# Cross-attention with a quantised feed-forward layer: three engines' attention loops written out, and each head's key loads cut in halves

## The chip, the cores and the metric

The kernel runs on one core of one Trainium2 chip. The core has five engines that work side by side, each with an instruction queue of its own: TensorE (PE in the profile) for matrix products, VectorE (DVE), ScalarE (ACT), GpSimd (POOL) and SyncE (SP), which here only issues DMAs. The engines wait for each other through semaphores. Sixteen DMA engines move data between DRAM and the on-chip memory, and they also do transposes on the way. The metric is the device time of one execution in microseconds (us). Less is better.

## The reference

With layer-normalised input x (4 x 512 tokens, 512 channels) and a context of 4 x 1601 = 6404 rows:

```python
q = (x @ Wq + bq).reshape(1, B * N, H, hd)            # 2048 queries, 16 heads of 32
kv = (cond @ Wkv + bkv).reshape(1, -1, 2, H, hd)      # 6404 keys and values
q = _fq_sym(q * scale, axis=-1)                       # to 8 bits and back, per query
k = _fq_sym(k, axis=-1)                               # per key
v = _fq_sym(v, axis=2)                                # per channel over all keys
attn = softmax(einsum('bhqd,bhkd->bhqk', q, k))
attn = _fq_unsigned(attn, axis=-1)                    # to 0..255 by the row's maximum, and back
out = einsum('bhqk,bhkd->bhqd', attn, v) @ Wp + bp
x = x + out
x = x + ffn(layernorm(x))                             # block-quantised, 512 -> 2048 -> 512
```

Every query attends to all 6404 keys.

## The kernel before

It has three stages: weights, queries, keys and values are made and written to DRAM; then `attention`; then `finish`, which is the output projection and the feed-forward layer. Only `attention` is changed.

**The unit of work** is a row: one head and one tile of 128 queries, against all 6404 keys. There are 16 heads (`H`) of 16 rows (`QT`), so 256 rows, and head h works on rows 16h to 16h + 15. Below, "row 5 of a head" counts from 0. What happens to a row:

1. TensorE makes the scores (L732), in five chunks (`NCH`) of 1280 or 1281 keys. The keys are held in three bf16 parts stacked to 96 partitions (`k_parts`, two slots: one for the head at work, one for the next), the queries likewise (`q_rep`).
2. VectorE copies each chunk out of the two PSUM buffers to `s_row` and takes its maximum in the same pass (L784). There are two `s_row` buffers, so row r + 2 waits until the exponents of row r are done.
3. GpSimd combines the five maxima and makes the bias of the exponent (L884 to L901).
4. ScalarE takes the exponent in two halves (L836): 3328 keys as bytes, 3076 as 16-bit integers.
5. SyncE issues two DMA transposes (`turn`): L711 for the byte half, L717 for the other.
6. GpSimd unpacks the transposed bytes in two casts (L909, L910), after it has done the maxima of the following row.
7. TensorE multiplies by the values (L745). This is put between the score chunks of the row three later (`LAG` = 3), in program order. ScalarE copies the result out (L842).

**Loads for the next head** are all issued by ScalarE, in `next_head`, between the exponents of its rows. `load` (L807 to L811) brings one of three key parts, all 6404 keys of 32 channels, and the queries for the same partitions; `load_values` brings the values in three pieces. Steps 0 to 2 (`load`) come in rows 2 to 4, steps 3 to 5 (`load_values`) in rows 5 to 7. Heads 1 to 14 do this for heads 2 to 15; heads 0 and 1 are loaded at the start, the values of head 1 in row 5 of head 0. TensorE's first row of a head waits for `head_loaded`, which counts 16 for each of six DMAs (L760). GpSimd scales and rounds the new values (`scale_values`, `round_values`) in three parts in its rows 8 to 13; TensorE waits for them in row 3 of their head (L765).

**Loops.** VectorE's part is written out in full. TensorE has one loop inside each head (L767), and that stays. ScalarE writes out heads 0, 1, 14 and 15 and loops over pairs of heads between (L871). GpSimd writes out head 0 and loops over pairs of heads, from an odd one on (L969), with a loop over the first eight rows inside (L939). SyncE loops over pairs of rows (L721). `settle` only increments a semaphore that nobody waits for.

Of the kernel before, what the change touches and what calls it, by code (L numbers as in the profile page):

```python
# [17 lines left out]
ds = bass.ds  # L18
# [601 lines left out]
def attention(nc, A, arena, q_dram, k_dram, v_dram, scales, v_scale, attn, zinv, wp, vectors, wp_loaded):  # L620
# [40 lines left out]
    VP = 3  # L661
# [3 lines left out]
    with Phase(nc, "a") as ph:  # L665
# [38 lines left out]
        def _(sp):  # L704
            def turn(pair, u):
                row = pair * 2 + u
                after_first(sp, unpacked, row - 1)
                settle(sp, sp_passed)
                sp.wait_ge(exp_done[0], row + 1)
                settle(sp, sp_passed)  # L710
# [3 lines left out]
                settle(sp, sp_passed)  # L714
                sp.wait_ge(exp_done[1], row + 1)
                settle(sp, sp_passed)
                sp.dma_start_transpose(nT[:, u, HALF_TILES:KT], n16[:, u, :].bitcast(FP16)).then_inc(turned[u][1], 16)  # L717

            turn(0, 0)
            turn(0, 1)  # L720
            with sp.Fori(1, PAIRS) as pair:  # L721
                for u in range(2):
                    turn(pair, u)

        @block.tensor
        def _(pe):
# [32 lines left out]
            def rows_of_head(h, slot, loaded):  # L759
                pe.wait_ge(head_loaded[slot], loaded * 96)  # L760
# [42 lines left out]
        def _(act):  # L803
# [18 lines left out]
            def next_head(h, slot, step):  # L822
# [22 lines left out]
            def rows_of_head(h, slot, last=False):  # L845
                for t in range(QT):
# [4 lines left out]
                    if not last and 2 <= t < 8 and not (isinstance(h, int) and h == 0):  # L851
                        next_head(h + 1, 1 - slot, t - 2)
# [5 lines left out]
            for s in range(3):  # L858
                load(0, 0, s)
# [3 lines left out]
            for s in range(3):  # L863
                load(1, 1, s)
# [15 lines left out]
        def _(pool):  # L880
            def take_scales(row, u):
                after_first(pool, exp_done[1], row - 1)
                settle(pool, pool_passed)
                nc.gpsimd.tensor_copy(row_scale[:, u, :], scales[:, row % QT, row // QT, :]).then_inc(scale_ready, 1)  # L884

            def maximum(row, u):
# [3 lines left out]
                settle(pool, pool_passed)  # L890
# [4 lines left out]
                settle(pool, pool_passed)  # L895
# [4 lines left out]
                settle(pool, pool_passed)  # L900
# [3 lines left out]
            def unpack(row, u):  # L904
# [3 lines left out]
                settle(pool, pool_passed)  # L908
# [8 lines left out]
            def scale_values(h, part):  # L917
                if part == 0:
                    pool.wait_ge(raw_loaded, h * 64 + 64)
                    settle(pool, pool_passed)  # L920
# [4 lines left out]
            def round_values(h, v_slot, part):  # L925
# [3 lines left out]
                settle(pool, pool_passed)  # L929
# [4 lines left out]
            PP = QT // 2  # L934
            BEFORE = 4

            def rows_of_head(h, slot):

                with pool.Fori(0, BEFORE) as i:  # L939
                    for u in range(2):  # L940
                        maximum_and_unpack(h * QT + (2 * i + u), u)
                for part in range(VP):
                    maximum_and_unpack(h * QT + 2 * (BEFORE + part), 0)
                    scale_values(h + 1, part)
                    maximum_and_unpack(h * QT + 2 * (BEFORE + part) + 1, 1)
                    round_values(h + 1, 1 - slot, part)
                for i in range(BEFORE + VP, PP):
                    for u in range(2):
                        maximum_and_unpack(h * QT + (2 * i + u), u)

            def first_rows():
                for row in range(2 * BEFORE):
                    maximum_and_unpack(row, row % 2)
                for part in range(VP):
                    maximum_and_unpack(2 * (BEFORE + part), 0)
                    scale_values(1, part)
                    maximum_and_unpack(2 * (BEFORE + part) + 1, 1)
                    round_values(1, 1, part)
# [514 lines left out]
```

## Time and profile before

| | |
|---|---|
| median of 3 runs | 2925.6 us |
| lowest, highest | 2914.03, 2931.51 us |
| the profiled execution | 2919.24 us |
| its span, first to last instruction | 2917.4 us |
| busy: VectorE, TensorE, ScalarE, GpSimd | 2513.0, 2268.8, 1993.3, 1400.3 us |
| DMA packets | 1420697, of them 1377512 under 512 B |

The profile comes from one execution. The span is cut into stretches or groups of instructions, and for each the busy time of an engine is given, and, in front of an instruction, how long its engine stood idle and what ended that. "Issue" means that it waited for nothing that the profile shows. The clock is the share of TensorE's full clock that was granted.

### The profile page before, as it was taken

The page shows a single profiled execution, that of the slowest core. Times are in us where ns is not written, and L with a number is a line of the kernel's source. Part 1 is how long each engine was busy: PE and PEld are TensorE (multiplying, and loading weights), DVE is VectorE, ACT ScalarE, POOL GpSimd, SP SyncE. Part 2 cuts the span into 40 slices and gives each one's busy share as a digit, 9 for nine tenths or more (in the row PEclk, how much of TensorE's full clock was granted, in tenths as well). Part 3 has the DMA queues.
Part 4 walks back from the last instruction along what each step waited for, and adds up shares of the span by engine and source line. Part 5 has one row for each costly group of instructions (what it writes and reads, how often), then busy time and mean ns, then how long its engine had stood idle before and what let it go on. Part 6 is the DMA issues. An engine that isn't in the chain of part 4 may idle for free. (4 is left out here: it accounts for less than half of the span.)

```text
span 2917.4 us, 58686 instructions
## 1 busy us (share of the span) xinstructions
PE 2268.8 (78%) x20020; PEld 1192.2 (41%) x20020; DVE 2513.0 (86%) x3665; ACT 1993.3 (68%) x1859; POOL 1400.3 (48%) x1772
## 2 busy tenths in 40 slices
PE   0379999976778788888778777878877888767876
PEld 0234555532444444444344444444434444433333
DVE  8665666657999999999899999999989999957887
ACT  1113444435888888888788888888878788855554
POOL 0001111114666657667576575765756667653331
PEclk9699999985887777777776678777778677888989
DMA  6112323338999999999999999999999999980000
GB/s 239 67 27 99 110 97 126 108 106 159 168 212 177 194 197 176 204 188 189 188 174 194 166 197 200 176 202 190 181 187 173 192 197 182 180 219 4 15 15 26
DMA packets 1420697, 444.96 MB, mean 153 GB/s; under 512 B 1377512, under 2 KB 1392872, under 8 KB 1417872
## 3 DMA queue, kind: packets, MB, share of 16 engines
q1 hardware_dynamic: 1311664, 402.10, 68.0%
q10 hardware_dynamic: 108864, 40.92, 7.6%
q8 instruction: 67, 1.10, 0.2%
q14 instruction: 102, 0.84, 0.1%
HBM read 80.41 MB, written 43.77 MB: 43 GB/s over the span
## 5 line engine op out<-in xcount | busy, mean ns | idle before, releaser
L784 DVE TENSOR_SCALAR_CACHE_REDUCE arena<-a_ps_s 128x1281 f32<-128x1281 f32 (+1 forms) x1280 | 1828.6, 1489 | 87.3 <-PE a_ps_s L732 53.5
L836 ACT ACTIVATE arena<-arena,a_bias,a_row_scale 128x3328 uint8<-128x3328 f32 (+1 forms) x512 | 1560.0, 3048 | 301.3 <-POOL a_bias L901 264.2
L732 PE MATMUL a_ps_s<-arena,a_q_rep 96*128 96x512 bf16 (+2 forms) x3840 | 1239.4, 445 | 345.3 <-DVE arena L784 316.8
L745 PEld LDWEIGHTS a_ps_o<-a_v_head,a_nT 128*128 128x128 f16 x13056 | 526.7, 103 | 340.8 <-issue 184.3
L909 POOL CAST a_nT<-arena 128x1664 int16<-128x1664 uint8 x256 | 401.8, 1569 | 521.4 <-DMA arena<-arena 501.0
L732 PEld LDWEIGHTS a_ps_s<-arena,a_q_rep 96*128 (+1 forms) x3840 | 316.2, 110 | 788.4 <-DVE arena L784 433.2
L745 PE MATMUL a_ps_o<-a_v_head,a_nT 128*128 128x32 f16 x13056 | 519.6, 184 | 77.0 <-POOL a_nT L910 59.7
L910 POOL CAST a_nT<-arena 128x1664 int16<-128x1664 uint8 x256 | 402.8, 1573 | 0.0
L471 POOL TENSOR_TENSOR kv_parts<-kv_rest,kv_parts 128x512 bf16<-128x512 f32 (+1 forms) x51 | 59.0, 1156 | 578.9 <-ACT kv_parts L586 578.9
L591 ACT ACTIVATE kv_stage<-kv_ps_t 128x1024 bf16<-128x1024 bf16 (+1 forms) x51 | 51.4, 1007 | 204.8 <-PE kv_ps_t L508 204.8
L499 PE MATMUL kv_ps_k<-wkv,kv_ctxT 128*128 128x512 f32 (+1 forms) x408 | 185.3, 597 | 0.0
L499 PE MATMUL kv_ps_v<-wkv,kv_ctxT 128*128 128x512 f32 (+1 forms) x408 | 183.4, 592 | 0.0
L896 POOL TENSOR_SCALAR a_row_max<-a_row_max,a_part_max 128x1 f32<-128x1 f32 x256 | 92.1, 360 | 85.8 <-POOL a_row_max L891 42.4
L499 PEld LDWEIGHTS kv_ps_v<-wkv,kv_ctxT 128*128 128x128 f32 (+1 forms) x408 | 76.7, 188 | 98.4 <-issue 98.4
L559 DVE TENSOR_TENSOR kv_rest<-kv_kq,kv_parts 128x512 f32<-128x512 f32 (+1 forms) x51 | 35.3, 692 | 81.9 <-issue 81.9
L784 DVE DVE_READ_ACCUMULATOR arena<-a_ps_s 128x1 f32 x1280 | 105.6, 83 | 0.0
L499 PEld LDWEIGHTS kv_ps_k<-wkv,kv_ctxT 128*128 128x128 f32 (+1 forms) x408 | 73.4, 190 | 75.0 <-issue 74.9
L930 POOL TENSOR_SCALAR a_v_head<-a_v_raw 128x544 f16<-128x544 f32 x48 | 98.6, 2055 | 0.0
L836 ACT ACTIVATION_READ_ACCUMULATOR arena<-arena,a_bias,a_row_scale (+1 forms) x512 | 95.9, 187 | 0.0
L901 POOL TENSOR_SCALAR a_bias<-a_row_max,a_row_scale 128x1 f32<-128x1 f32 x256 | 66.6, 260 | 59.3 <-POOL a_row_max L896 58.6
L891 POOL TENSOR_SCALAR a_row_max<-a_part_max 128x1 f32<-128x1 f32 x256 | 93.2, 364 | 0.5
L369 PE MATMUL w_ps_t<-ident,arena 128*128 128x128 bf16 x128 | 12.3, 289 | 86.3 <-DVE arena L293 86.3
(157 smaller groups left out, 1946.5 us busy)
## 6 DMA issues: line engine op xcount, KB each, us to landing
arena<-k_parts_transposed ACTq DMA_DIRECT2D x48, 400.2 KB, 4.9
k_parts_transposed<-kv_stage SPq DMA_DIRECT2D x10, 1920.0 KB, 7.9
kv_ctx<-in_ctx_dram SPq DMA_DIRECT2D x10, 1280.0 KB
v<-arena SPq DMA_DIRECT2D x10, 1280.0 KB
arena<-in_L_ffn_W_dram SPq DMA_DIRECT2D x2, 4096.0 KB, 20.8
a_v_raw<-v ACTq DMA_DIRECT2D x32, 208.0 KB
a_q_rep<-q_transposed ACTq DMA_DIRECT2D x48, 128.0 KB, 5.8
a_v_raw<-v ACTq DMA_DIRECT2D x16, 384.0 KB
```

Of the source, the lines that this page charges most:

```text
L471: nc.gpsimd.tensor_tensor(parts[0:r, 2, :], rest1[0:r, :], parts[0:r, 1, :], ALU.subtract).then_inc(lo_ready, 1)
L499: last = nc.tensor.matmul(ps[0:r, u, :], ctxT[:, u, j, 0:r], wkv[:, j, col:col + C], start=(j == 0), stop=(j == CC - 1))
L732: last = nc.tensor.matmul(ps_s[:, b, n0:n0 + w], q, k_parts[0:3 * HD, slot, start[c] + n0:start[c] + n0 + w], start=True, stop=True)
L745: last = nc.tensor.matmul(ps_o[:, u, 0:HD], nT[:, u, j, :], v_head[:, v_slot, j, :], start=(j == 0), stop=(j == KT - 1))
L784: nc.vector.tensor_scalar(s_row[:, u, start[c]:start[c] + size[c]], ps_s[:, (u + c) % 2, 0:size[c]], 1.0, None, ALU.mult, ALU.max, accum_o ...
L836: nc.scalar.activation(out, s_row[:, u, keys_of_half[half]], ACT.Exp, scale=row_scale[:, u, 0:1], bias=bias[:, u:u + 1], accum_out=zsum[:, ...
L891: nc.gpsimd.tensor_scalar(m, part_max[:, u, 0:1], part_max[:, u, 1:2], part_max[:, u, 2:3], ALU.max, ALU.max).then_inc(three_done, 1)
L896: nc.gpsimd.tensor_scalar(m, m, part_max[:, u, 3:4], part_max[:, u, 4:5], ALU.max, ALU.max).then_inc(row_max_ready, 1)
L901: nc.gpsimd.tensor_scalar(bias[:, u:u + 1], row_max[:, u:u + 1], row_scale[:, u, 1:2], LN255, ALU.mult, ALU.add).then_inc(bias_ready, 1)
L909: nc.gpsimd.tensor_copy(low_T[u], bytes_T[:, u, :, 0])
L910: nc.gpsimd.tensor_copy(high_T[u], bytes_T[:, u, :, 1]).then_inc(unpacked, 1)
L930: nc.gpsimd.tensor_scalar(v_head[:, v_slot, part * VT:(part + 1) * VT, :], v_raw[:, part * VT:(part + 1) * VT, :], ROUND, ROUND, ALU.add, ...
```

## The change

The loops of ScalarE, GpSimd and SyncE in `attention` are replaced by plain Python loops, so that every row's instructions are written out, and the `settle` calls there go. `load` now moves one key part in two DMAs, keys 0 to 2561 (`MIDDLE` = `start[2]` = 2562) and keys 2562 to 6403; the queries go with the second. The six halves are issued in rows 0 to 5 of a head, one a row, and the three value loads in rows 6 to 8. `head_loaded` therefore counts nine DMAs (144). GpSimd's work on the values goes from rows 8 to 13 to rows 10 to 15 (`BEFORE` = 10).

```diff
             def turn(pair, u):
                 row = pair * 2 + u
                 after_first(sp, unpacked, row - 1)
-                settle(sp, sp_passed)
                 sp.wait_ge(exp_done[0], row + 1)
-                settle(sp, sp_passed)
...
-            turn(0, 0)
-            turn(0, 1)
-            with sp.Fori(1, PAIRS) as pair:
+            for pair in range(PAIRS):
                 for u in range(2):
                     turn(pair, u)
...
-                pe.wait_ge(head_loaded[slot], loaded * 96)
+                pe.wait_ge(head_loaded[slot], loaded * 144)
...
-            def load(h, slot, s):
-                act.dma_start(k_parts[s * HD:(s + 1) * HD, slot, :],
-                             k_dram[s, ds(h * HD, HD), :]).then_inc(head_loaded[slot], 16)
+            MIDDLE = start[2]
+
+            def load(h, slot, s, half):
+                keys = slice(0, MIDDLE) if half == 0 else slice(MIDDLE, K)
+                act.dma_start(k_parts[s * HD:(s + 1) * HD, slot, keys],
+                             k_dram[s, ds(h * HD, HD), keys]).then_inc(head_loaded[slot], 16)
+                if half == 0:
+                    return
                 act.dma_start(q_rep[s * HD:(s + 1) * HD, slot, :],
                              q_dram[ds(h * HD, HD), :]).then_inc(head_loaded[slot], 16)
...
                 if step == 0:
                     act.wait_ge(scores_ready, (h - 1) * (QT * NCH))
-                if step < 3:
-                    load(h, slot, step)
-                if step >= 3:
+                if step < 6:
+                    load(h, slot, step // 2, step % 2)
+                if step >= 6:
                     act.wait_ge(v_rounded, h * VP)
-                    load_values(h, step - 3)
+                    load_values(h, step - 6)
...
-                    if not last and 2 <= t < 8 and not (isinstance(h, int) and h == 0):
-                        next_head(h + 1, 1 - slot, t - 2)
+                    if not last and t < 9 and not (isinstance(h, int) and h == 0):
+                        next_head(h + 1, 1 - slot, t)
...
             for s in range(3):
-                load(0, 0, s)
+                for half in range(2):
+                    load(0, 0, s, half)
...
-            rows_of_head(0, 0)
-            rows_of_head(1, 1)
-            with act.Fori(1, H // 2 - 1) as hh:
-                for slot in range(2):
-                    rows_of_head(2 * hh + slot, slot)
-            rows_of_head(H - 2, 0)
-            rows_of_head(H - 1, 1, last=True)
+            for h in range(H):
+                rows_of_head(h, h % 2, last=(h == H - 1))
...
-            BEFORE = 4
-
-            def rows_of_head(h, slot):
-
-                with pool.Fori(0, BEFORE) as i:
...
+            BEFORE = 10
+
+            def rows_of_head(h):
+
+                for t in range(QT):
+                    maximum_and_unpack(h * QT + t, t % 2)
+                    part = (t - BEFORE) // 2
+                    if h + 1 < H and 0 <= part < VP:
+                        if t % 2 == 0:
+                            scale_values(h + 1, part)
+                        else:
+                            round_values(h + 1, (h + 1) % 2, part)
...
-            with pool.Fori(0, H // 2 - 1) as hh:
-                rows_of_head(2 * hh + 1, 1)
-                rows_of_head(2 * hh + 2, 0)
-            with pool.Fori((H - 1) * PP, H * PP) as pair:
-                for u in range(2):
-                    maximum_and_unpack(2 * pair + u, u)
+            for h in range(H):
+                rows_of_head(h)
             unpack(ROWS - 1, 1)
```

## Rows read from the trace of the kernel before

"..." marks rows left out. A timeline row is: start, duration (us), engine, line, operation, output <- input, count, and in brackets the idle time before it and what ended it. In rows of L784 alone the columns are: stretch, its length, VectorE's busy time, clock, DMA share, GB/s; the sum adds the stretches' lengths.

**Rows 1.** head of the page: span, and busy time of each engine

```profile
span 2917.4 us, 58686 instructions
PE 2268.8 (78%) x20020; PEld 1192.2 (41%) x20020; DVE 2513.0 (86%) x3665; ACT 1993.3 (68%) x1859; POOL 1400.3 (48%) x1772
```

**Rows 2.** stretches: us, busy us by engine, TensorE clock, DMA share, GB/s

```profile
...
662.90:2580.50 1917.60, 1526.34 (x16788) 821.33 (x16788) 1830.27 (x2561) 1592.71 (x1272) 1224.14 (x1626) 0.75 1.02 186
...
```

**Rows 3.** costliest groups by line

```profile
L784 DVE TENSOR_SCALAR_CACHE_REDUCE arena<-a_ps_s 128x1281 f32<-128x1281 f32 (+1 forms) x1280 | 1828.6, 1489 | 87.3 <-PE a_ps_s L732 53.5
L836 ACT ACTIVATE arena<-arena,a_bias,a_row_scale 128x3328 uint8<-128x3328 f32 (+1 forms) x512 | 1560.0, 3048 | 301.3 <-POOL a_bias L901 264.2
...
```

**Rows 4.** L784 alone, one stretch per head (head 15, and the sum of sixteen)

```profile
...
2466.47:2580.44 113.97, 113.71 (x162) 0.85 0.96 177
sum 1917.54, DVE 1830.21; mean DVE 114.39
```

**Rows 5.** L784 alone, rows 5 to 7 of heads 1 to 14

```profile
...
2139.96:2170.84 30.88, 21.62 (x31) 0.61 1.12 185
...
sum 355.45, DVE 302.47; mean DVE 21.61
```

**Rows 6.** L784 alone, rows 8 to 15 of heads 1 to 14

```profile
...
sum 804.61, DVE 799.98; mean DVE 57.14
```

**Rows 7.** L784 alone, row 1 of heads 3, 5, 7, 9, 11, 13

```profile
...
sum 50.34, DVE 43.05; mean DVE 7.18
```

**Rows 8.** timeline of head 12, row 2, and of VectorE three rows later

```profile
2131.94 1.60 SPq L711 DMA_TRANSPOSE arena<-arena  x1
2132.18 0.38 ACTq L808 DMA_DIRECT2D arena<-k_parts_transposed  x1
2134.87 6.54 SPq L717 DMA_TRANSPOSE a_nT<-arena  x1
2141.14 1.57 POOL L909 CAST a_nT<-arena 128x1664 int16<-128x1664 uint8 x1 [7.02 <-DMA arena<-arena]
...
2146.09 1.49 DVE L784 TENSOR_SCALAR_CACHE_REDUCE arena<-a_ps_s 128x1281 f32<-128x1281 f32 x1 [3.22 <-PE a_ps_s L732]
```

**Rows 9.** timeline: a row without loads, then one with value loads

```profile
1490.77 1.47 SPq L711 DMA_TRANSPOSE arena<-arena  x1
...
1494.78 1.57 POOL L909 CAST a_nT<-arena 128x1664 int16<-128x1664 uint8 x1 [1.25 <-DMA arena<-arena]
...
2414.61 0.37 ACTq L818 DMA_DIRECT2D a_v_raw<-v  x1
2414.92 1.98 SPq L711 DMA_TRANSPOSE arena<-arena  x1
...
2420.65 1.57 POOL L909 CAST a_nT<-arena 128x1664 int16<-128x1664 uint8 x1 [2.70 <-DMA arena<-arena]
```

**Rows 10.** DMA issues: count, KB each, us from issue to landing

```profile
arena<-k_parts_transposed ACTq DMA_DIRECT2D x48, 400.2 KB, 4.9
a_q_rep<-q_transposed ACTq DMA_DIRECT2D x48, 128.0 KB, 5.8
a_v_raw<-v ACTq DMA_DIRECT2D x16, 384.0 KB
```

**Rows 11.** timeline of head 5: GpSimd in its row 0, VectorE in row 2

```profile
1275.06 0.18 POOL L884 COPY a_row_scale<-scales 128x2 f32 x1 [3.38 <-issue]
...
1280.21 1.49 DVE L784 TENSOR_SCALAR_CACHE_REDUCE arena<-a_ps_s 128x1281 f32<-128x1281 f32 x1 [0.57 <-ACT arena L836]
```

**Rows 12.** timeline: first loads, first scores, VectorE's first stall

```profile
650.39 0.41 ACTq L808 DMA_DIRECT2D arena<-k_parts_transposed  x1
...
652.75 0.44 ACTq L810 DMA_DIRECT2D a_q_rep<-q_transposed  x1
...
660.23 1.04 PE L732 MATMUL a_ps_s<-arena,a_q_rep 96*128 96x512 bf16 x2 [19.70 <-DMA a_q_rep<-q_transposed]
...
691.89 1.49 DVE L784 TENSOR_SCALAR_CACHE_REDUCE arena<-a_ps_s 128x1281 f32<-128x1281 f32 x1 [14.76 <-ACT arena L836]
```

More of the change, by code:

```diff
@@ L863, in _ @@
             for s in range(3):
-                load(1, 1, s)
+                for half in range(2):
+                    load(1, 1, s, half)
             act.dma_start(wp[:], A.wp.rearrange("(j p) n -> p j n", p=P)).then_inc(wp_loaded, 16)
@@ L882, in take_scales @@
                 after_first(pool, exp_done[1], row - 1)
-                settle(pool, pool_passed)
                 nc.gpsimd.tensor_copy(row_scale[:, u, :], scales[:, row % QT, row // QT, :]).then_inc(scale_ready, 1)
@@ L889, in maximum @@
                 pool.wait_ge(scores_taken, row * NCH + 3)
-                settle(pool, pool_passed)
                 nc.gpsimd.tensor_scalar(m, part_max[:, u, 0:1], part_max[:, u, 1:2], part_max[:, u, 2:3],
@@ L894, in maximum @@
                 pool.wait_ge(three_done, row + 1)
-                settle(pool, pool_passed)
                 nc.gpsimd.tensor_scalar(m, m, part_max[:, u, 3:4], part_max[:, u, 4:5],
@@ L899, in maximum @@
                 pool.wait_ge(scale_ready, row + 1)
-                settle(pool, pool_passed)
                 nc.gpsimd.tensor_scalar(bias[:, u:u + 1], row_max[:, u:u + 1], row_scale[:, u, 1:2], LN255,
@@ L907, in unpack @@
                 after_first(pool, values_done, row - 1)
-                settle(pool, pool_passed)
                 nc.gpsimd.tensor_copy(low_T[u], bytes_T[:, u, :, 0])
@@ L919, in scale_values @@
                     pool.wait_ge(raw_loaded, h * 64 + 64)
-                    settle(pool, pool_passed)
                 tiles_of = v_raw[:, part * VT:(part + 1) * VT, :]
@@ L928, in round_values @@
                     pool.wait_ge(values_done, (h - 1) * QT)
-                settle(pool, pool_passed)
                 nc.gpsimd.tensor_scalar(v_head[:, v_slot, part * VT:(part + 1) * VT, :],
@@ L932, in round_values @@
                                         ALU.add, ALU.subtract).then_inc(v_rounded, 1)
-            PP = QT // 2
-            BEFORE = 4
-            def rows_of_head(h, slot):
-                with pool.Fori(0, BEFORE) as i:
-                    for u in range(2):
[L941 to L958, printed above, removed]
-                for row in range(2 * (BEFORE + VP), QT):
-                    maximum_and_unpack(row, row % 2)
+            BEFORE = 10
[8 more added lines that the diff above has]
+                            round_values(h + 1, (h + 1) % 2, part)
             nc.gpsimd.partition_all_reduce(v_scale[:], v_scale[:], P, bass.bass_isa.ReduceOp.max).then_inc(reduced, 1)
@@ L967, in _ @@
                 round_values(0, 0, part)
-            first_rows()
-            with pool.Fori(0, H // 2 - 1) as hh:
-                rows_of_head(2 * hh + 1, 1)
-                rows_of_head(2 * hh + 2, 0)
-            with pool.Fori((H - 1) * PP, H * PP) as pair:
-                for u in range(2):
-                    maximum_and_unpack(2 * pair + u, u)
+            for h in range(H):
+                rows_of_head(h)
             unpack(ROWS - 1, 1)
```

2 lines of the change are left out of this document (removed).

## Prediction

> **What bounds the kernel now.** I read the head of the page first [rows 1], then cut the execution into stretches. The attention stage, from VectorE's first to its last L784, holds 1917.60 of 2917.4 us, and VectorE is busy in it for 1830.27 [rows 2]. Only this stage is changed. Its work is 1280 passes of L784, five for each of 256 rows, and all the idle time in front of them is 87.3 us [rows 3]. ScalarE is next, with 3.05 us for each of two exponents a row. So the change can win back what VectorE idles, and no more, and the question is where those 87 us lie.
>
> For that I cut the stage by rows. Rows 8 to 15 of heads 1 to 14, 112 rows, take 804.61 us, 7.184 each [rows 6]. Head 15, during which nothing is loaded for a next head, takes 113.97, or 7.12 a row [rows 4]. That is the pace without trouble. Three places are off it:
>
> - Rows 5 to 7 of heads 1 to 14: 42 rows in 355.45 us. At 7.184 they would take 301.7, so 53.7 us are lost, 1.28 a row. In head 12 alone the three rows take 30.88 [rows 5].
> - Row 1 of the six odd heads from 3 to 13: 50.34 us for 43.1, so 7.2 lost [rows 7].
> - The start, once: VectorE waits 14.76 us for the first exponent [rows 12].
>
> **Why rows 5 to 7 are late.** ScalarE issues the three key loads in its rows 2, 3 and 4. The timeline of head 12 shows what one does. The byte transpose (L711) starts at 2131.94, the key load (L808) 0.24 us later, and GpSimd's unpack (L909), which waits for that transpose, starts at 2141.14: 9.20 us instead of the 4.01 of a row without loads [rows 8, 9]. The second transpose's issue is held for 6.54 us too. TensorE does this row's values between the scores three rows later (LAG = 3), in order, so the scores are late and VectorE waits 3.22 us [rows 8]. The DMA share of the stage is 1.02 [rows 2]: there is hardly a gap in which a load could hide. From that pair of numbers the transposes may be late by 9.20 - 3.22 - 4.01 = 1.97 us before VectorE feels it. The lost 1.28 us a row then mean a mean lateness of about 3.25 us in a key-load row.
>
> Value loads are issued in rows 5 to 7, and would hurt in rows 8 to 10, where nothing is lost [rows 6]. The largest, 384 KB [rows 10], gives 2420.65 - 2414.92 = 5.73 us from transpose to unpack [rows 9], 1.72 over the quiet row and inside the allowance.
>
> **Part 1, key loads in halves.** Before, each of three rows carries 400.2 + 128.0 = 528 KB of keys and queries [rows 10]. MIDDLE is 2562 of 6404 keys. Now rows 0, 2, 4 carry 160 KB and rows 1, 3, 5 carry 240 + 128 = 368 KB. I take lateness as proportional to bytes. Light rows: 0.30 x 3.25 = 1.0 us, inside the allowance, cost nothing. Heavy rows: 0.70 x 3.25 = 2.3 us, 0.3 over. The lateness varies, though. The worst first load, in head 12, has 9.20 - 4.01 = 5.19 us [rows 8, 9], which becomes 3.6 and loses 1.7, while mild ones lose nothing. I take 0.45 us for each of 42 heavy rows: 19 us left of 53.7, a gain of 35. The bounds: the value load of 384 KB lost nothing, so 368 KB may lose nothing either, a gain of 53.7; or the same bytes lose the same time wherever they lie, a gain of 0.
>
> A rule of the Trainium skill speaks against the halves: "DMA: Bandwidth & Descriptors", section "Bandwidth", says to batch DMAs and that small ones are inefficient, and its section on the anatomy of one DMA gives a fixed part of about 2.0 us each (for those issued by GpSimd). Estimated from that page, 42 more DMAs are 84 us of transfer time, and were all of it on the path, the sum would end near 2962 and not near 2880. The rows show a whole 400 KB load landing in 4.9 us [rows 10], with VectorE at work meanwhile.
>
> **Part 2, no loops on GpSimd, ScalarE and SyncE.** In row 0 of head 5 GpSimd stands 3.38 us before L884 for no reason but issue, exactly where the loop over pairs of heads (L969) goes round; the exponents are late behind it, and VectorE waits 0.57 [rows 11]. Six heads show this, for 7.2 us together [rows 7]. Straight code has no such turn: -7.2. Its upper bound is that, its lower bound 0 if the pause comes again as a fetch of straight code. Against a pause in straight code: VectorE runs all its 1280 passes so, and of its 87.3 us of idle time [rows 3] the three places above explain 53.7 + 7.2 + 14.8, leaving 12 for 1280 passes. The removed settles (a semaphore increment each) stand on engines that wait for VectorE or the DMA anyway, GpSimd being busy 1224 of 1917.6 us [rows 2]: 0, covered by VectorE's passes; without that cover leaving them out could only gain. SyncE has run no long straight code here, so its term is bounded by 0 and by GpSimd's 3.38 us per pause, of which the allowance of 1.97 hides most; I take 0.
>
> **Part 3, values two rows later.** The three value loads go from ScalarE's rows 5 to 7 to 6 to 8, the scaling and rounding on GpSimd from rows 8 to 13 to rows 10 to 15. The rounded values are needed at row 3 of the next head (L765), more than two rows (14 us) after the last of them. Of the same work in the same kind of rows nothing is lost now [rows 6]: 0. ScalarE issues DMAs in nine rows a head and not in six, in light rows only one; its share of busy time, 1592.71 of 1917.6 us [rows 2], leaves 1.27 us a row, and the two issues of a heavy row take 0.38 + 0.44 [rows 8, 12].
>
> **Part 4, the start.** Head 0 now issues nine DMAs before the value loads. Six take 652.75 - 650.39 + 0.44 = 2.8 us, 0.47 each [rows 12]. Scores wait for the last query load, and the first exponent for the value loads behind it, so three more cost 1.4 us: +1.4. Between 0 and 2.8 if the issue of head 1's loads counts as well.
>
> **Sum.** -35 - 7.2 + 1.4 = -40.8 us against the profiled execution, 2919.24 us, of which 2917.4 are the span. That gives 2878. The median of the three runs is 2925.6, 6.4 above; I can't tell why, and if it is by more late transposes, the change takes those too; from there the sum gives 2885. I say 2880.
>
> **The rivals.** (a) All late rows vanish (0.20): 368 KB behaves as 384 KB of values do. Then -53.7 - 7.2 + 1.4 = -59.5, 2860 to 2866. Against it: by the code a value load moves pieces of 128 B and a key load pieces of 5 to 8 KB, and long pieces may hold up a transpose more than short ones. (b) Lateness follows the bytes however they are cut (0.16): the queue is full, so six rows lose what three lost. Then -5.8: 2913 to 2920. For it speaks the DMA share of 1.02; against it the value loads: 6404 x 32 x 4 bytes, 820 KB in three rows, follow the keys at once and lose nothing [rows 6]. (c) Slower (0.09): a key-load row loses 1.28 us whatever its size, because 32 key rows must pass between the transposes in each. Then 84 rows lose 107.4 us, +53.7 - 7.2 + 1.4 = +47.9: 2967 to 2974. It decides from 0.71 us per load row on ((53.7 + 5.8) / 84). The trace has key loads of one size only, so nothing there excludes it; the value loads, which also come in pieces over all engines, lose nothing, and speak against a price that any load pays. The forecast itself has 0.55, its own range 2868 to 2896.
>
> The range for eight in ten reaches from (a) to (b), 2858 to 2920; only (c) is outside. Half a per cent, 15 us, is about what measurement can tell from no change. Faster by more: the forecast, (a), and a small part of (b), 0.77; within: 0.14; slower: 0.09.
>
> **What would show it.** In the profile after: rows 3 to 8 of heads 1 to 14 lose about 19 us together, in rows 4, 6 and 8 (three after the heavy loads) and not 3, 5, 7; from byte transpose to unpack about 6.3 us in heavy rows, 5 in light ones; row 1 of odd heads at 7.1 to 7.2; the stage near 1877 us; rows 10 to 15 at 7.18. Wrong would be: pauses for issue on SyncE, GpSimd or ScalarE in front of L711, L884 or L836 in many rows; TensorE waiting at L765; or light rows as late as heavy ones.

## The result and the profile after

The changed kernel takes 2849.61 us (median of 4 runs, 2847.96 to 2854.95), the kernel before in the same comparison 2927.15 (4 runs, 2914.03 to 2931.51). The ratio is 0.9746, with a 95% interval of 0.9711 to 0.9780: faster, by 77.5 us. The forecast was 2880 with a range of 2858 to 2920. The direction was right, the size was not: the time lies 8 us below the low end of the range, and below what the most hopeful rival gave.

The page of the changed kernel, head, costliest groups and DMA issues:

```profile
span 2846.7 us, 54272 instructions
...
PE 2213.0 (78%) x20003; PEld 1185.6 (42%) x20020; DVE 2507.0 (88%) x3665; ACT 1993.3 (70%) x1859; POOL 1403.7 (49%) x1772
...
L778 DVE TENSOR_SCALAR_CACHE_REDUCE arena<-a_ps_s 128x1281 f32<-128x1281 f32 (+1 forms) x1280 | 1822.9, 1489 | 26.0 <-PE a_ps_s L726 10.6
L835 ACT ACTIVATE arena<-arena,a_bias,a_row_scale 128x3328 uint8<-128x3328 f32 (+1 forms) x512 | 1559.8, 3047 | 242.9 <-POOL a_bias L893 201.9
...
arena<-k_parts_transposed ACTq DMA_DIRECT2D x48, 240.1 KB, 3.8
...
arena<-k_parts_transposed ACTq DMA_DIRECT2D x48, 160.1 KB, 3.8
...
a_q_rep<-q_transposed ACTq DMA_DIRECT2D x48, 128.0 KB, 5.3
```

VectorE's 1280 passes are L778 now and not L784. They take 1822.9 us, 5.7 less than before, and the idle time in front of them is 26.0 us where it was 87.3 [rows 3]. So nearly all is in what VectorE waited for. The stage as one stretch:

```profile
660.10:2510.10 1850.00, 1475.38 (x16790) 814.73 (x16788) 1824.01 (x2561) 1592.73 (x1274) 1227.40 (x1626) 0.80 1.05 193
```

It is 1850.0 us long, 67.6 less than before [rows 2]. And cut by rows, L778 alone: first rows 5 to 7 of heads 1 to 14, second rows 3 to 8 of these heads (the rows that stand three behind a key load now), third their rows 9 to 15, fourth row 1 of the odd heads from 3 to 13. In each answer the sum stands last:

```profile
sum 306.73, DVE 299.29; mean DVE 21.38
...
sum 612.56, DVE 599.19; mean DVE 42.80
...
sum 699.95, DVE 697.86; mean DVE 49.85
...
sum 42.50, DVE 42.49; mean DVE 7.08
```

The same three stretches of the kernel before, where they were not shown yet (rows 3 to 8, rows 9 to 15):

```profile
sum 656.80, DVE 601.73; mean DVE 42.98
...
sum 704.18, DVE 700.21; mean DVE 50.02
```

From two such sums comes the measure that I use from here on. **Lost** is what the 84 rows 3 to 8 of heads 1 to 14 take above the pace of the 98 rows 9 to 15, in which nothing is late. Before: 656.80 - 84 x 704.18 / 98 = 53.2 us. After: 612.56 - 84 x 699.95 / 98 = 12.6. The 77.5 us are made up as follows, from the two profiled executions:

| where | before | after | difference |
|---|---|---|---|
| late rows ("lost") | 53.2 | 12.6 | -40.6 |
| row 1 of six odd heads | 50.34 | 42.50 | -7.8 |
| VectorE's first stall | 14.76 | 5.55 | -9.2 |
| rest of the stage (the pace falls from 7.186 to 7.142 us a row: 256 x 0.044 = 11) | | | -10.0 |
| ahead of the stage and behind it | 999.8 | 996.7 | -3.1 |
| span | 2917.4 | 2846.7 | -70.7 |

The remaining 7 us are that the profiled execution of before was 8 us faster than the median of its runs, and that of after 1 us faster. The first row is what I had forecast for part 1, within 6 us. The third had a term of the wrong sign, +1.4 (part 4), and the last two, 13 us, had none. Of these 13 us the experiments explain nothing: in a second profile of the changed kernel (g3 below) the pace is 7.163 us a row and not 7.142. It will turn out that the first row isn't what it seems either.

### The profile page after: what moved, and what is told of

It is laid out like the page before. It is cut to its first block and busy times, and to the rows that moved or that the text cites. A ratio compares the mean times of both kernels' runs of the same rounds, so it can differ in the third digit from the quotient of the medians.

```text
span 2846.7 us, 54272 instructions
## 1 busy us (share of the span) xinstructions
PE 2213.0 (78%) x20003; PEld 1185.6 (42%) x20020; DVE 2507.0 (88%) x3665; ACT 1993.3 (70%) x1859; POOL 1403.7 (49%) x1772
## 5 line engine op out<-in xcount | busy, mean ns | idle before, releaser
L778 DVE TENSOR_SCALAR_CACHE_REDUCE arena<-a_ps_s 128x1281 f32<-128x1281 f32 (+1 forms) x1280 | 1822.9, 1489 | 26.0 <-PE a_ps_s L726 10.6
L726 PE MATMUL a_ps_s<-arena,a_q_rep 96*128 96x512 bf16 (+2 forms) x3840 | 1186.6, 429 | 378.5 <-DVE arena L778 345.9
L726 PEld LDWEIGHTS a_ps_s<-arena,a_q_rep 96*128 (+1 forms) x3840 | 309.0, 108 | 809.5 <-DVE arena L778 460.5
L739 PE MATMUL a_ps_o<-a_v_head,a_nT 128*128 128x32 f16 x13056 | 512.6, 182 | 26.2 <-POOL a_nT L901 23.6
L559 DVE TENSOR_TENSOR kv_rest<-kv_kq,kv_parts 128x512 f32<-128x512 f32 (+1 forms) x51 | 35.3, 692 | 81.9 <-issue 81.9
L778 DVE DVE_READ_ACCUMULATOR arena<-a_ps_s 128x1 f32 x1280 | 106.3, 83 | 0.0
L835 ACT ACTIVATION_READ_ACCUMULATOR arena<-arena,a_bias,a_row_scale 128x1 f32 x512 | 95.8, 187 | 0.0
```

The lines of the kernel that those rows point to most:

```text
L726: last = nc.tensor.matmul(ps_s[:, b, n0:n0 + w], q, k_parts[0:3 * HD, slot, start[c] + n0:start[c] + n0 + w], start=True, stop=True)
L739: last = nc.tensor.matmul(ps_o[:, u, 0:HD], nT[:, u, j, :], v_head[:, v_slot, j, :], start=(j == 0), stop=(j == KT - 1))
L778: nc.vector.tensor_scalar(s_row[:, u, start[c]:start[c] + size[c]], ps_s[:, (u + c) % 2, 0:size[c]], 1.0, None, ALU.mult, ALU.max, accum_o ...
L835: nc.scalar.activation(out, s_row[:, u, keys_of_half[half]], ACT.Exp, scale=row_scale[:, u, 0:1], bias=bias[:, u:u + 1], accum_out=zsum[:, ...
```

## The experiments

Unless something else is said, a kernel is the changed one with the edit shown. "Before" is always the kernel before, run in the same comparison on the same chip. The last column is the mean time from the end of a row's last score pass on VectorE to the issue of its byte transpose, over rows 0 to 5 of heads 1 to 14.

| kernel | median us | before | ratio (95%) | first stall | lost | scores' end to transpose |
|---|---|---|---|---|---|---|
| before | 2927.15 | | | 14.76 | 53.2 | 7.61 |
| after | 2849.61 | 2927.15 | 0.9746 (0.9711 to 0.9780) | 5.55 | 12.6 | 5.59 |
| e1_loops_only | 2880.36 | 2918.17 | 0.9863 (0.9817 to 0.9910) | 5.37 | 35.3 | 5.71 |
| e2_loads_only | 2887.37 | 2918.17 | 0.9870 (0.9827 to 0.9912) | 12.9 | 30.8 | 7.25 |
| e3_whole_spaced | 2891.49 | 2918.17 | 0.9890 (0.9850 to 0.9929) | 5.58 | 47.7 | 6.56 |
| e4_queries_first | 2845.58 | 2918.17 | 0.9738 (0.9700 to 0.9775) | 5.02 | 2.0 | 5.24 |
| f5_settles_kept | 2871.51 | 2924.02 | 0.9830 (0.9789 to 0.9871) | 12.54 | 17.7 | 5.96 |
| f6_pool_loops | 2870.14 | 2924.02 | 0.9824 (0.9784 to 0.9864) | 13.63 | 14.2 | 5.77 |
| f7_act_loop | 2859.26 | 2924.02 | 0.9788 (0.9748 to 0.9827) | 5.07 | 20.0 | 6.20 |
| f8_sync_loop | 2857.73 | 2924.02 | 0.9775 (0.9735 to 0.9816) | 5.84 | 22.1 | 5.94 |
| g1_one_settle | 2860.24 | 2922.12 | 0.9797 (0.9754 to 0.9839) | 12.38 | 15.2 | 5.64 |
| g2_row_settles_twice | 2871.08 | 2922.12 | 0.9840 (0.9796 to 0.9885) | 6.04 | 25.8 | 6.39 |
| g3_after_again | 2852.59 | 2922.12 | 0.9770 (0.9737 to 0.9802) | 5.38 | 8.8 | 5.48 |
| g4_queries_first_again | 2844.48 | 2922.12 | 0.9746 (0.9713 to 0.9779) | 5.19 | 10.6 | 5.40 |
| h3_quiet_start | 2854.26 | 2929.16 | 0.9742 (0.9706 to 0.9777) | 5.24 | 9.0 | 5.46 |

The measure "lost" comes from one profiled execution each. The same kernel gave 12.6 and 8.8 (after and g3), and another 2.0 and 10.6 (e4 and g4): differences of less than about 8 us in it say nothing by themselves. e1, e2 and e3 are less than 2% under the kernel before, but their intervals lie clear of 1.

### Each half of the change alone: e1_loops_only, e2_loads_only

e1 has all loops written out and no settles, with the loads as before: whole key parts in rows 2 to 4, values in rows 5 to 7 and 8 to 13.

> The loops of ScalarE, GpSimd and SyncE written out and settle gone, loads as before: whole key parts in rows 2 to 4, values in rows 5 to 7, six DMAs a head. Theory L (the cut loads did nearly all of it): rows 5 to 7 of heads 1 to 14 still lose about 54 us, only row 1 of the odd heads comes back, 7 us, so the time is 2913 to 2921 beside 2927 before. Theory C (ScalarE's straight code also makes key loads milder, as in heads 1 and 14 of the kernel before, which are straight on ScalarE and lost 0.8 and 2.0 us in these rows where the looped heads lost 4.4 on average): rows 5 to 7 lose about 20 us, and the time is 2875 to 2895. Either: the first stall of VectorE tells whether the start came from the loops (5 to 6 us) or from the loads (14 to 15 us).

e2 is the kernel before, with its loops and settles, and the new loads: halves in rows 0 to 5, values two rows later.

> Loops and settle as before, loads as after: halves in rows 0 to 5, values in rows 6 to 8. Theory L: the late rows lose 10 to 15 us, row 1 of the odd heads still 7 us, time 2857 to 2865. Theory C: the looped heads keep half of their lateness, 25 to 35 us, time 2870 to 2885. My prediction's own sum for this alone was -34 us, 2893.

e1 is 37.8 us under before and e2 30.8. Together 68.6, against 69.5 to 77.5 for the whole change: the two halves of the change add up within what the runs can tell, and neither needs the other. This contradicts the prediction's shares, -7.2 for the loops and about -34 for the loads. The sums of e2, rows 3 to 8 and then 9 to 15:

```profile
sum 635.92, DVE 600.99; mean DVE 42.93
...
sum 706.02, DVE 700.30; mean DVE 50.02
```

And of e1:

```profile
sum 637.18, DVE 601.55; mean DVE 42.97
...
sum 702.19, DVE 698.94; mean DVE 49.92
```

By the same working e2 loses 30.8 us and e1 35.3. So the halves won 22 of the 53 late us and not 35, and writing out the loops and dropping the settles, priced at nothing in these rows, won 18.

The traces say how. Call a load row's *lateness* what its byte transpose takes to the unpack above 4.0 us, and its *allowance* the lateness less what the row three later loses against the pace. e2 and the changed kernel have the same loads, and their transposes are equally late: in rows 1, 3 and 5 it is 6.44, 6.53 and 6.20 us to the unpack in e2, and 6.15, 6.99 and 6.20 in the changed kernel. The allowance differs. Its median, over those of rows 0 to 5 of heads 1 to 14 whose third row later loses more than 0.5 us (few, 8 to 26 in a kernel), is 1.8 us in the kernel before and 1.9 in e2, and 2.3 in e1, 2.6 in e3 and in the changed kernel, and 2.7 in g3. So the cut loads make transposes less late, and the written-out code lets them be later. e1 also has the short first stall, and e2 keeps the long one: the start belongs to the loops and settles too.

Row 1 of the six odd heads takes 42.88 us in e1, and 43.63 in e2, which still has GpSimd's loops. So the 7.2 us of part 2 go with either half of the change. I come back to this at f6.

### Size or spacing: e3_whole_spaced, e4_queries_first, g4_queries_first_again

e3 loads whole parts of 400 KB with the queries, but only in every second row:

```diff
-                if step < 6:
-                    load(h, slot, step // 2, step % 2)
+                if step < 6 and step % 2 == 0:
+                    load(h, slot, step // 2)
```

> As after, but key parts whole with their queries, 528 KB, in rows 0, 2 and 4, nothing in rows 1, 3, 5. Size theory (lateness follows the bytes of one row): rows 3, 5, 7 lose about 1.3 us each as before, 42 rows, 54 us less what came from one load falling into the lateness of another (about 12 us): time 2880 to 2892. Spacing theory (it is the three loads in successive rows that hurt): within 6 us of after, 2850 to 2856.

e4 sends the queries with the first, smaller half. The rows then carry 288 and 240 KB in turn, and not 160 and 368:

```diff
-                if half == 0:
+                if half == 1:
                     return
```

> As after, but the queries go with the first half, so rows carry 288 and 240 KB instead of 160 and 368 KB. Size theory: lateness at most 0.55 x 3.25 = 1.8 us on average, inside the allowance of 1.97 us, so less is lost than in after: 2840 to 2848. Number theory (a row pays for the number of DMAs, two against one): the losses only move from rows 4, 6, 8 to rows 3, 5, 7, and the time stays within 4 us of after.

Where the rows lose, as sums over the sixteen heads of what each row took above 7.075 us:

| row of the head | 3 | 4 | 5 | 6 | 7 | 8 |
|---|---|---|---|---|---|---|
| before: 528 KB in rows 2, 3, 4 | 2.0 | 1.2 | 36.6 | 9.4 | 16.3 | 1.7 |
| e1: the same, no loops | 1.4 | 1.7 | 10.8 | 17.8 | 13.4 | 2.1 |
| e3: 528 KB in rows 0, 2, 4 | 16.2 | 2.1 | 18.9 | 2.0 | 18.9 | 2.0 |
| after: 368 KB in rows 1, 3, 5, 160 KB in 0, 2, 4 | 1.4 | 4.7 | 1.1 | 7.6 | 4.8 | 3.3 |
| g3, the same again | 0.8 | 6.1 | 1.2 | 5.3 | 5.1 | 2.0 |
| e4: 288 KB in rows 0, 2, 4, 240 KB in 1, 3, 5 | 0.9 | 0.8 | 1.8 | 2.0 | 5.4 | 2.5 |

The losses stand three rows behind the loads in every kernel, and move when the loads move: the chain from transpose to scores over `LAG` = 3 is right. (Some 4 us of row 7 belong to head 0, where head 1's values are loaded at once.) Spacing alone gains nothing. e3 loses 47.7 us, 1.14 for each of its 42 load rows, more than e1 (35.3). Cutting the load does it: 368 KB lose 12.6 / 42 = 0.3 us for each load row, 288 and 240 KB less still (2.0 and 10.6 us in all in its two profiles). Rows 5 to 7 of e3, one stretch per head (the last seven heads):

```profile
1651.18:1672.59 21.41, 21.38 (x33) 0.84 1.11 212
1767.49:1790.82 23.33, 21.57 (x31) 0.65 1.08 202
1884.39:1905.80 21.41, 21.36 (x31) 0.84 1.15 203
1998.89:2022.51 23.62, 21.68 (x31) 0.57 1.09 186
2118.22:2144.83 26.61, 21.50 (x31) 0.68 1.02 189
2240.41:2264.06 23.65, 21.44 (x31) 0.70 1.06 212
2357.12:2380.42 23.30, 21.39 (x33) 0.78 1.05 205
sum 333.25, DVE 301.02; mean DVE 21.50
```

One head loses nothing, the next 2 to 5 us, with the same loads: the lateness varies as the prediction said, and the allowance cuts off its lower part.

e4 is the fastest kernel of the study, and was run again beside the changed kernel:

> The changed kernel itself once more, on the chip and beside the runs of this call, as a yardstick: 2847 to 2855.

> The queries with the first half once more, beside the changed kernel. Size theory: 3 to 7 us below it, 2843 to 2847. Number theory: the same within 2 us.

2844.48 (2841.30 to 2848.41) against 2852.59 (2848.06 to 2854.28), six runs each: 8 us less. That even loads win this in the late rows isn't shown. In these two profiles the late rows lose 10.6 and 8.8 us, and the attention stage is only 2.1 us shorter (1847.1 against 1849.2); the other 6.7 us lie ahead of it and behind it, where the two kernels are the same.

### Which of the removed instructions: f5 to f8

Each of these puts one piece back into the changed kernel: f5 all settles, on GpSimd and SyncE, without loops; f6 GpSimd's loops with its settles; f7 ScalarE's loop over pairs of heads; f8 SyncE's loop over pairs of rows with its settles.

> As after, all three engines straight, but with the settle calls back (five a row on GpSimd, four on SyncE). The runs before this one show that the loops alone gave 38 us, and that late rows and start came down with them. Theory G1 (the semaphore increments delay GpSimd's chain from the last score to the bias, and so every transpose behind it): bias about 1 us later in quiet rows than in after, late rows lose 25 to 35 us, time 2865 to 2880. Theory G2 (it is the loops' registers, not the increments): within 5 us of after, 2846 to 2855.

> As after, but GpSimd with its loops and settles as before (BEFORE = 5 pairs, the same rows 10 to 15), ScalarE and SyncE straight. If GpSimd carries what the loops cost, all of it is back: row 1 of the odd heads 7 us, start stall 13 to 15 us instead of 5.5, late rows 30 to 36 us, so near the kernel with all loops and the new loads, 2880 to 2895. If ScalarE or SyncE carry it: only the 7 us of row 1, 2855 to 2860.

> As after, but ScalarE with its loop over pairs of heads, GpSimd and SyncE straight. Theory S (register addresses in ScalarE's loop make key loads worse, as heads 1 and 14 of before suggest): heads 2 to 13 lose 2 to 3 us each in late rows, 2865 to 2880. If GpSimd carries it: within 5 us of after, 2846 to 2856.

> As after, but SyncE with its loop over pairs of rows and its settles, ScalarE and GpSimd straight. A transpose was issued 0.20 us after its exponents in before and 0.12 in after; if only this returns, 0.1 us less allowance in a row costs 2 to 5 us: 2848 to 2856. If SyncE's loop is what made transposes late, late rows lose 25 us or more: above 2865.

Their gains over before are 52.5, 53.9, 64.8 and 66.3 us. No single piece brings back all of the 35 us by which e2, with all of them, is slower than the changed kernel (g3). These four ran without the changed kernel beside them, and its gains in its own two comparisons were 77.5 and 69.5 us: that f5 and f6 gain less is clear, for f7 and f8 the difference is near what the runs can tell.

**The first stall** is short in f7 and f8 and long in f5 and f6. These two share GpSimd's settles and nothing else, so the settles make it. In the late rows f5 and f6 lose 17.7 and 14.2 us, which one profile each can hardly tell from 12.6 and 8.8.

**GpSimd's loop** doesn't cost what I priced it at. In f6 the loop over pairs of heads is there, and row 1 of the odd heads takes 42.76 us, as without it. Where the loop goes round, before the first instruction of head 5, GpSimd in f6 doesn't stop at all, while in the kernel before it stood 3.38 us there [rows 11]:

```profile
1257.08 1.58 POOL L906 CAST a_nT<-arena 128x1664 int16<-128x1664 uint8 x1
1258.63 2.06 POOL L926 TENSOR_SCALAR a_v_head<-a_v_raw 128x544 f16<-128x544 f32 x1
1260.63 0.19 POOL L880 COPY a_row_scale<-scales 128x2 f32 x1
```

In f6 and e2 the rounding of the values is the last thing before the turn, and the loop's body is two written-out rows a head shorter. Either may be the reason, and no run tells them apart. That a taken branch out of the fetched window costs a fetch is what the Trainium skill says ("Runtime: NRT & Kernel Launch", section "Instruction fetch mechanics"); the six pauses of before, 2.3 to 4.0 us each, agree in kind, and the same branch in e2 and f6 with no pause in front of L880 and its like shows that it may be hidden.

**SyncE's and ScalarE's loops** lose 22.1 and 20.0 us in the late rows, against 12.6 and 8.8. In both the transpose comes later after the scores, 5.94 and 6.20 us against 5.59 and 5.48. ScalarE's loop has pauses of its own: in f7 there is one of 2.39 us before row 0 of head 4 and one of 4.05 before row 0 of head 10, where the loop goes round, and these are the two heads whose late rows lose most (3.8 and 4.8 us). That the pauses make the loss isn't shown.

```profile
1137.49 3.16 ACT L835 ACTIVATE arena<-arena,a_bias,a_row_scale 128x3328 uint8<-128x3328 f32 x1 [2.39 <-issue]
```

### What a settle costs: g1_one_settle, g2_row_settles_twice

g1 puts back a single settle, in `scale_values`. It is executed once for each head, and only the first, at the start, is on the path:

```diff
                 if part == 0:
                     pool.wait_ge(raw_loaded, h * 64 + 64)
+                    settle(pool, pool_passed)
```

> As after, with one settle only, the one in scale_values between the wait for the values' landing and GpSimd's first scaling (it runs once a head). In the runs so far VectorE's first stall is 5 to 6 us without GpSimd's settles and 12.7 to 14.8 us with them. If this settle is the cause, the first scaling starts 6 to 9 us later than in after and the time is 2855 to 2859; late rows as in after. If the start goes with something else in the settles of the rows, the stall stays at 5 to 6 us and the time within 3 us of after.

g2 puts two settles at each of five places of every row on GpSimd (`take_scales`, three in `maximum`, `unpack`) and none in `scale_values`:

```diff
                 pool.wait_ge(scores_taken, row * NCH + NCH)
                 pool.wait_ge(three_done, row + 1)
+                settle(pool, pool_passed)
+                settle(pool, pool_passed)
                 nc.gpsimd.tensor_scalar(m, m, part_max[:, u, 3:4], part_max[:, u, 4:5],
```

> As after, with two settles at each of the five places of a row on GpSimd, none at the start of the scaling and none on SyncE. One at each place made the time from the copy of the scales to the end of the bias 1.59 us against 1.44, and with SyncE's the late rows lose about 12 us more. Headroom theory (each tenth of a us in the chain from the last score to the transpose takes allowance from key-load rows): copy to bias 1.7 to 1.8 us, late rows lose 25 us or more beyond after, start as in after, 2870 to 2890. If late rows do not care for this chain: within 5 us of after.

Beside g3 (2852.59) in the same comparison, g1 takes 7.7 us more and g2 18.5 more. Of what g1 adds, 7.0 us are in the start; its late rows lose 15.2 us against 8.8, which is within what the measure can't tell. GpSimd in g1, the maximum over partitions and the first scaling:

```profile
656.36 1.80 POOL L937 PARTITION_ALL_REDUCE v_scale<-v_scale  x1 [16.47 <-issue]
672.48 3.91 POOL L913 TENSOR_TENSOR a_v_raw<-a_v_raw,a_inv 128x544 f32<-128x544 f32 x3 [14.32 <-issue]
```

The changed kernel, without the settle, up to the end of VectorE's first stall:

```profile
652.49 1.81 ACTq L814 DMA_DIRECT2D a_v_raw<-v  x2
...
654.55 1.80 POOL L936 PARTITION_ALL_REDUCE v_scale<-v_scale  x1 [16.44 <-issue]
...
656.85 3.35 DVE L788 RECIPROCAL a_inv<-v_scale 128x512 f32<-128x512 f32 x1
...
658.22 2.85 ACTq L819 DMA_DIRECT2D a_v_raw<-v  x1
...
660.12 1.43 DVE L778 TENSOR_SCALAR_CACHE_REDUCE arena<-a_ps_s 128x1281 f32<-128x1281 f32 x1
...
663.83 3.93 POOL L912 TENSOR_TENSOR a_v_raw<-a_v_raw,a_inv 128x544 f32<-128x544 f32 x3 [7.48 <-issue]
...
679.89 1.50 DVE L778 TENSOR_SCALAR_CACHE_REDUCE arena<-a_ps_s 128x1281 f32<-128x1281 f32 x1 [5.55 <-ACT arena L835]
```

From L936 to L912 it is 663.83 - 654.55 = 9.3 us; in g1 it is 16.1. GpSimd's first bias waits behind this scaling, the first exponent for the bias, and VectorE, which has only two row buffers, for the exponent. So the 6.8 us come out whole in the first stall, 12.38 against 5.38 in g3. The kernel before had 18.4 us there and a stall of 14.76 [rows 12]. "Issue" in the bracket is the same word in both: the profile can't say what the settle waits for.

g2 shows the other cost. GpSimd's bias chain of one row in the changed kernel:

```profile
1483.49 0.19 POOL L879 COPY a_row_scale<-scales 128x2 f32<-128x2 f32 x1
1483.66 0.38 POOL L885 TENSOR_SCALAR a_row_max<-a_part_max 128x1 f32<-128x1 f32 x1
1484.21 0.36 POOL L889 TENSOR_SCALAR a_row_max<-a_row_max,a_part_max 128x1 f32<-128x1 f32 x1 [0.17 <-POOL a_row_max L885]
1484.67 0.26 POOL L893 TENSOR_SCALAR a_bias<-a_row_max,a_row_scale 128x1 f32<-128x1 f32 x1
```

And in g2:

```profile
1470.19 0.19 POOL L881 COPY a_row_scale<-scales 128x2 f32<-128x2 f32 x1
1470.36 0.38 POOL L889 TENSOR_SCALAR a_row_max<-a_part_max 128x1 f32<-128x1 f32 x1
1471.01 0.36 POOL L895 TENSOR_SCALAR a_row_max<-a_row_max,a_part_max 128x1 f32<-128x1 f32 x1 [0.27 <-POOL a_row_max L889]
1471.68 0.26 POOL L901 TENSOR_SCALAR a_bias<-a_row_max,a_row_scale 128x1 f32<-128x1 f32 x1 [0.31 <-POOL a_row_max L895]
```

From the copy to the end of the bias it is 1.44 us without settles and 1.75 with two at each place; the kernel before, with one, has 1.58. Three of the five places lie between these two points, so six settles cost 0.31 us and three 0.14: 0.05 us each, in a row in which VectorE waits for nothing. The late rows do notice: their loss is 25.8 us in g2 against 8.8 in g3, 17 us more, and the median time is 18.5 more (the two profiled executions are 13.1 apart). The median allowance, 2.7 us in g3, is 2.2 in g2. So settles on one engine, with nothing else changed, raise the late rows' loss. In the table, "lost" and the last column rise together, by and large, among the kernels with the new loads, from 5.24 us and 2.0 to 7.25 us and 30.8. By itself that column proves little, since a late row also makes the next transposes late; it is g2, where only settles were added, that gives the direction. The way from the settles to the allowance isn't shown in full. In the quiet rows 9 to 14 of these heads the time in the column is 5.61 us in g2 and in g3 alike: the bias is 0.4 us later on average, but ScalarE takes it up 0.15 us after its end and not 0.49. In e2 it is 6.71 there, and none of f5 to f8 comes above 5.77. So the settles and the loops do more together than any one of them, and that part stays open.

### Why the settle at the start is dear: h1 to h3

Two ideas: the settle is slow because the DMA engines are busy with other transfers then, or because of what it stands behind. h1 has g1's settle ahead of the wait for the values and not behind it. h2 and h3 take the competing transfers away: head 1's keys are loaded in rows 7 to 12 of head 0, and `wp` and the vectors in head 15; h2 has g1's settle, h3 has not.

> As g1_one_settle, with the one settle ahead of the wait for the values' landing, so that the wait stands directly before the scaling again. If the place behind the wait is what costs, the first scaling starts as in after, some 9 us after the all-reduce, and VectorE's first stall is 5 to 6 us. If any settle there costs, it starts about 16 us after, and the stall is 12 to 13 us.

> The settle behind the wait as in g1, but the key loads of head 1 go from the start to rows 7 to 12 of head 0, and the loads of Wp and the vectors to row 2 of head 15. If the settle costs because of DMA traffic at that moment, the scaling starts within 10 us of the all-reduce and the first stall is below 7 us; if it costs by itself, 16 us and 12 to 13 us as in g1.

> As h2, without the settle. The scaling starts as in after, about 9 us after the all-reduce, or up to 3 us earlier if the traffic held the values; the moved key loads may cost a few us in rows 10 to 15 of head 0. Within 4 us of after: 2846 to 2855.

h1 (one run, 2856.25 us) has 12.8 us from L937 to the scaling and a first stall of 9.05: about half the cost. h3's and h2's GpSimd, in this order:

```profile
654.95 1.80 POOL L936 PARTITION_ALL_REDUCE v_scale<-v_scale  x1 [16.52 <-issue]
663.94 1.32 POOL L912 TENSOR_TENSOR a_v_raw<-a_v_raw,a_inv 128x544 f32<-128x544 f32 x1 [7.19 <-DMA a_v_raw<-v]
```

```profile
655.04 1.80 POOL L937 PARTITION_ALL_REDUCE v_scale<-v_scale  x1 [16.41 <-issue]
670.43 1.33 POOL L913 TENSOR_TENSOR a_v_raw<-a_v_raw,a_inv 128x544 f32<-128x544 f32 x1 [13.59 <-issue]
```

In h3 the scaling is released by the DMA of the values, at 663.94. In h2 it comes 6.5 us later. The DMA engines of h2 between 652 and 676 us, in forty slices of 0.6 us:

```profile
DMA  9997999999999469950000000000000000000000
```

They are silent from about 662.8 on, in h2 as in h3. So the values had landed, nothing else was in flight, and the settle still cost its 6.5 us (2860.57 us, one run, against 2854.26 for h3; first stall 11.65 against 5.24). Traffic is excluded by this run; the place matters, by about half, as far as h1's one run tells; what the settle waits for stays open. Taking the traffic away (h3, against the changed kernel) wins nothing.

## Why the prediction was too small, point by point

**Part 1, key halves (-35, range of the part 0 to -53.7).** The mechanism holds: three rows behind the load, lateness above an allowance, growing with the size of one row's load. The losses stand in rows 4, 6 and 8 as forecast. The size was too high for this half taken alone: e2 loses 30.8 us and not 19 (0.73 for each of 42 heavy rows, forecast 0.45), so it gave -22. The lateness was forecast well: in the kernel before it is 3.2 us on average in rows 2 to 4 (forecast 3.25). From byte transpose to unpack the changed kernel's rows 1, 3 and 5 take 6.15, 6.99 and 6.20 us on average (forecast 6.3), and rows 0, 2 and 4 5.47, 4.88 and 4.74 (forecast 5). The light one of head 10, row 2, follows its heavy one:

```profile
1839.92 1.55 SPq L709 DMA_TRANSPOSE arena<-arena  x1
...
1847.75 1.57 POOL L900 CAST a_nT<-arena 128x1664 int16<-128x1664 uint8 x1 [4.86 <-DMA arena<-arena]
1848.38 1.52 SPq L709 DMA_TRANSPOSE arena<-arena  x1
...
1852.59 1.57 POOL L900 CAST a_nT<-arena 128x1664 int16<-128x1664 uint8 x1 [0.38 <-DMA arena<-arena]
```

7.83 us and 4.21. The allowance of 1.97 us, taken from the one pair 9.20 and 3.22 of head 12, was right for the kernel before (median 1.8), but by luck. In that same row VectorE waits a second time, behind the other transpose, which I left out; the row takes 14.63 us and not 7.2, and loses more than its byte transpose is late:

```profile
2153.11 1.49 DVE L784 TENSOR_SCALAR_CACHE_REDUCE arena<-a_ps_s 128x1280 f32<-128x1280 f32 x1 [4.11 <-PE a_ps_s L732]
```

And the allowance is no constant of the kernel. It is what the rest of the row leaves over, and it was 2.6 us when the loops and settles had gone.

**The failed step: "The removed settles (...) stand on engines that wait for VectorE or the DMA anyway (...): 0", and with it SyncE's term of 0.** This cover is real in a quiet row, and it was no cover in the late rows and at the start. In the late rows the settles and loops eat from the allowance, 1.9 us with all of them (e2) against 2.6: 30.8 us lost with them, 12.6 and 8.8 with none, and 25.8 when settles alone are added, two at each place (g2). At the start GpSimd is itself on the path, where a single settle costs 7.0 us of stall (g1). The sum of -40.8 missed the profiled difference of -70.7 by 30 us: in the late rows the loops and settles gave 18 us that I had at nothing and the halves 13 less than forecast, together 5.6; the start gave 9.2 instead of costing 1.4; part 2 gave 0.6 more; and 13 lie in the pace and outside the stage, with no cause shown.

**Part 2, the pause of GpSimd's loop (-7.2).** Measured: 50.34 to 42.50, -7.8. The number was right, the reason was only half so: e1 wins it without the loops, e2 with them (43.63).

**Part 3, values later (0).** Held: rows 9 to 15 take 699.95 us, no more than before. I had costed a row's two DMA issues at 0.38 and 0.44, though, and the last value load (L819) holds ScalarE's queue for 3.55 us in row 8 of head 2, with the exponent 2.95 late behind it. VectorE is two rows of buffers ahead and doesn't notice.

**Part 4, the start (+1.4).** The nine issues do take longer, from 648.27 to 652.49, 4.2 us where six took 2.8 [rows 12]. No cost of it shows. VectorE's first pass (660.12) comes right after the reciprocal (656.85 + 3.35), which needs the values' maximum and not these loads. The first exponent does wait for the value loads, as I had it: h3 names their DMA as what ends GpSimd's wait. But from the first load's issue to the scaling it is 15.6 us in the changed kernel and 15.7 in e1, which issues six: the third value load (L817) held ScalarE's queue for 3.86 us, and for 5.32 in e1. The first stalls are 5.55 and 5.37 us. So the chain was right, and of the 1.4 us about 0.2 show.

**The rivals.** (a), all late rows vanish, came nearest: the loss is down to a quarter. But it was to come by the size alone, and by e2 size alone leaves 30.8 us. (b), the same bytes lose the same time, is refuted by e3 beside the changed kernel: the same bytes per head, 47.7 us lost and 12.6. (c), a price for any load row, by the light rows: three behind them rows 3 and 5 lose 1.4 and 1.1 us over sixteen heads, and e4, with a middling load in each of six rows, loses 2.0 and 10.6 us in all, where (c) asks for 107. The rule weighed in the prediction ("DMA: Bandwidth & Descriptors" in the Trainium skill, section "Bandwidth": batch DMAs) would have put the time near 2962; no cost of the 42 DMAs more shows here: with the new loads alone (e2) the kernel is 30.8 us faster.

## What to carry to other kernels

Where a stall is cut off by an allowance, price every instruction in the chain that feeds the allowance, even those that stand on an idle engine: here settles that make one chain 0.31 us longer in a quiet row cost 17 us over the late ones. And take the allowance from many rows, not from one. Where bulk loads share the DMA engines with transposes that something waits for, cut the loads to pieces, one piece a row; spacing without cutting gained nothing, and that even pieces win more isn't shown. And look for the one place, mostly the start, where the idle engine is not idle.

## What the runs showed of the hardware

- A semaphore increment by itself on GpSimd, between a wait and the instruction behind it, cost 6.5 to 7 us at the start (g1, and h2, where the DMA engines were silent), and 0.05 us in the bias chain of a row (g2). Why the two differ is open.
- A plain load on ScalarE's queue delays a DMA transpose on SyncE's, the more the larger it is. From issue to unpack it is 4.0 us in a quiet row (median), and on average 5.7 and 6.1 us in rows with 240 and 288 KB (e4), 6.4 with 368 KB (the changed kernel) and 7.2 with 528 KB (before).
- Written-out code on SyncE, GpSimd and ScalarE showed no pause at the places where the loops had been, though the kernel has 256 rows of it. ScalarE's remaining pauses, up to 3.1 us before the exponent of row 9 and one of 7.6 in head 0, stand behind value loads, as in part 3.
- TensorE's granted clock went with the lateness. In the three-row stretches of e3 shown above it is 0.84 of 2.4 GHz where no row is late and 0.57 to 0.78 where rows are, and over the stage it is 0.75 before and 0.80 after. TensorE waits more in late rows; whether the lower clock adds to the lateness wasn't tried.
